# Attention and feed-forward block: TensorE takes over the last sum, GpSimd weighs two rows, gathers follow the transposes

## What is computed

```python
x = x + xattn(layernorm(x), ctx, idx, Wq, Wkv, Wo)
x = x + ffn(layernorm(x), w_gate, w_up, w_down)

def xattn(q, kv_src, seg_id, Wq, Wkv, Wo):      # 16 heads of 32
    qh = heads(q @ Wq.T)
    k, v = split(kv_src @ Wkv.T)                # 154 rows per batch
    gather = seg_id[:, :, None] - arange(4)     # 4 rows of the table per query
    k_sel, v_sel = k[clip(gather)], v[clip(gather)]
    scores = where(gather < 0, lowest, (qh * k_sel).sum(-1) / sqrt(32))
    probs = softmax(scores, over the 4 rows)
    return (probs * v_sel).sum(over the 4 rows) @ Wo.T
```

## Time and profile before

| what | us |
|---|---|
| median of 3 runs | 2348.56 |
| lowest, highest | 2347.93, 2349.85 |
| span of the profiled execution | 2347.3 |
| TensorE busy in it | 2020.4 (86%) |
| VectorE busy | 1715.7 (73%) |
| ScalarE busy | 1398.2 (60%) |
| GpSimd busy | 670.6 (29%) |

### The profile page before, as it was taken

How to read it: one execution, slowest core, us unless ns; L and a number is a source line. 1 busy time by engine, 2 the same in 40 slices (tenths; PEclk the granted TensorE clock), 3 DMA queues, 4 the chain that set the end, 5 groups by cost and what they waited for, 6 DMA issues and landing times.

```text
span 2347.3 us, 25386 instructions
## 1 busy us (share of the span) xinstructions
PE 2020.4 (86%) x9524; PEld 945.0 (40%) x9524; DVE 1715.7 (73%) x1387; ACT 1398.2 (60%) x1599; POOL 670.6 (29%) x662
## 2 busy tenths in 40 slices
PE   5888888888599999999999999999000699999998
PEld 2444444444244444444444444444000344444443
DVE  8799999999634534532499998999899644577641
ACT  4678887887422322322499996676899633366530
POOL 2599999998300000000121110222111000000000
PEclk9999999999799999999999999999555899999999
DMA  7789999998346656743699995787998755555541
GB/s 297 283 314 337 348 337 346 335 350 316 126 181 226 225 207 223 259 148 144 242 378 390 378 369 209 264 320 293 401 419 327 291 229 208 205 201 232 233 152 72
DMA packets 131162, 634.60 MB, mean 270 GB/s; under 512 B 12256, under 2 KB 12768, under 8 KB 91104
## 3 DMA queue, kind: packets, MB, share of 16 engines
q1 hardware_dynamic: 85888, 316.81, 37.0%
q0 software_dynamic: 45152, 316.16, 34.6%
HBM read 430.69 MB, written 202.24 MB: 270 GB/s over the span
## 4 chain that ended last, share of the span: by engine, by line
PE 64%; issue 3%; DVE 3%; ACT 2%; POOL 0%; DVEq 0%; ACTq 0%; POOLq 0%
PE fd_pp L1777 42%; PE fd_pp L1791 21%; ACT ff_ring L1720 1%; DVE ff_sig L1575 1%; DVE ff_h_parts L1559 1%; DVE ff_sq L1497 1%; ACT ff_sig L1707 0%; DVE ff_sq L1566 0%; DVE kept_gate L1568 0%; DVE ff_gin L1510 0%; DVE ff_hq L1549 0%; ACT ff_hq L1632 0%; ACT ff_ring L1746 0%; ACT ff_sig L1736 0%; DVE kept_o_peak L1575 0%
## 5 line engine op out<-in xcount | busy, mean ns | idle before, releaser
L1791 PE MATMUL fd_pp<-ff_down,kept_gate 128*128 128x512 f16 x1536 | 458.9, 381 | 193.1 <-DVE ff_up L1616 193.1
L1777 PE MATMUL fd_pp<-ff_h_parts,kept_gate 128*128 128x512 f16 x2304 | 499.6, 380 | 14.3 <-DVE ff_h_parts L1415 14.3
L1777 PE MATMUL fd_pp<-ff_h_parts,ff_up 128*128 128x512 f16 x2304 | 497.4, 379 | 0.0
L1639 ACT ACTIVATE ff_raw<-fd_pp 128x1024 f32<-128x1024 f32 x192 | 194.3, 1017 | 396.5 <-PE fd_pp L1777 396.5
L1777 PEld LDWEIGHTS fd_pp<-ff_h_parts,kept_gate 128*128 128x128 f16 x2304 | 225.9, 98 | 287.9 <-DVE ff_h_parts L1415 14.7
L1777 PEld LDWEIGHTS fd_pp<-ff_h_parts,ff_up 128*128 128x128 f16 x2304 | 225.4, 98 | 271.8
L1420 DVE TENSOR_REDUCE kept_gate_peak<-ff_raw 128x1 f32<-128x2048 f32 x48 | 109.7, 2285 | 292.9 <-ACT ff_raw L1639 292.9
L1791 PEld LDWEIGHTS fd_pp<-ff_down,kept_gate 128*128 128x128 f16 x1536 | 150.6, 98 | 375.9 <-issue 195.8
L1791 PE MATMUL fd_pp<-ff_down,ff_up 128*128 128x512 f16 x768 | 292.2, 380 | 0.0
L1746 ACT ACTIVATE ff_ring<-ff_hq,kept_g 128x2048 int16<-128x2048 f32 x48 | 96.0, 1999 | 191.1 <-DVE ff_hq L1549 189.7
L790 PE MATMUL at_psO<-kept_wo,at_ahi 128*128 128x512 f16 x512 | 155.5, 386 | 36.2 <-ACT at_alo L277 31.6
(11 more groups left out here) (239 smaller groups left out, 3454.9 us busy)
## 6 DMA issues: line engine op xcount, KB each, us to landing
ff_raw<-up_scratch SPq DMA_DIRECT2D x66, 1024.0 KB, 8.5
gate_scratch<-ff_raw POOLq DMA_DIRECT2D x48, 1024.0 KB, 9.1
ff_gin<-gate_scratch SPq DMA_DIRECT2D x48, 1024.0 KB, 8.7
up_scratch<-ff_raw POOLq DMA_DIRECT2D x48, 1024.0 KB, 7.7
ff_gin<-gate_integers SPq DMA_DIRECT2D x73, 512.0 KB, 5.8
gate_integers<-ff_ring POOLq DMA_DIRECT2D x43, 512.0 KB, 8.7
ff_up<-up_scratch SPq DMA_DIRECT2D x21, 1024.0 KB, 9.5
kept_xs<-in_x SPq DMA_DIRECT2D x32, 512.0 KB, 14.6
```

The source lines that it names most:

```text
L1639: nc.scalar.activation(raw[:, n % UNITS, h * 2 * BLK:(h + 1) * 2 * BLK], pp[(2 * n + h) % 4][:, :, :].rearrange("p a t -> p (a t)"), ACT.C ...
L1777: mm = nc.tensor.matmul(pp[k % 4][:, h, :], wt[w][:, c, f:f + P], a[:, b % 2, :, c, :], start=(q == 0), stop=(q == len(todo) - 1))
L1791: mm = nc.tensor.matmul(pp[k % 8 // 2][:, k % 2, :], a[b % 2][:, f, t * P:(t + 1) * P], wt[w][:, f, :], start=(q == 0 and i == 0), stop=(q ...
```

## The change

Five things change in `opening`:

- VectorE weighs rows 0 and 1 only (1024 numbers instead of 1536). GpSimd weighs rows 2 and 3 (`weigh_upper`, 1024 numbers instead of 512), still once both tiles of the pair are weighed by VectorE.
- The second sum and its buffer `att` are gone (a buffer `room` keeps the place in memory). TensorE turns both half sums into the same place in PSUM, eight transposes instead of four, the second four accumulating on the first.
- The semaphore `att` is gone. TensorE waits for `half`; SyncE and the gathers wait for `aT`, so a buffer is gathered into once TensorE has turned its tile.
- GpSimd issues the gather for the even tile before the norm's four instructions, and the one for the odd tile behind them.
- For the last pair VectorE only makes the first sum (`add_last`).

The diff:

```diff
--- before.py
+++ after.py
@@ -158,7 +158,8 @@
 
         xn = r.sb("xn", [P, 2, D], F32)
         xhi, xlo = (r.sb(n, [P, 2, DC, P], F16) for n in ("xhi", "xlo"))
-        att, hn = (r.sb(n, [P, 2, D], F32) for n in ("att", "hn"))
+        r.sb("room", [P, 2, D], F32)
+        hn = r.sb("hn", [P, 2, D], F32)
         hT = r.sb("hT", [P, 4, D], F32)
         ahi, alo = (r.sb(n, [P, 2, DC, P], F16) for n in ("ahi", "alo"))
         kv = r.sb("kv_rows", [P, KR, W, 2 * D], F32)
@@ -185,7 +186,7 @@
         x1_out = [r.sem(f"x1_out{i}") for i in range(XR)]
         hT_out = [r.sem(f"hT_out{i}") for i in range(2)]
         rows_in = [r.sem(f"rows_in{i}") for i in range(KR)]
-        m = r.sems("xn xT xhi xrest xlo q prod raw sc top ds ex tot inv pr pv last half att aT ahi arest alo o x1 "
+        m = r.sems("xn xT xhi xrest xlo q prod raw sc top ds ex tot inv pr pv last half aT ahi arest alo o x1 "
                    "nmean ssq ssq_v stat aggr sqe root rstd norm x_nmean x_ssq hn hT hT_sb peak h_red h_all reduced")
 
         def blocks(t, h):
@@ -232,7 +233,7 @@
                         sp.dma_start(x1_v[p], xs[:, ring(p), :]).then_inc(x1_out[p % XR], 16)
                     p = s_ - 5
                     if p == NP - 6:
-                        sp.wait_ge(m["att"], KR * (NT // KR) - KR + 6 if NT % KR == 0 else NT - NT % KR)
+                        sp.wait_ge(m["aT"], KR * (NT // KR) - KR + 6 if NT % KR == 0 else NT - NT % KR)
                         for b in range(2):
                             sp.wait_ge(hT_out[0], 16 * (b + 1))
                             sp.wait_ge(hT_out[1], 16 * (b + 1))
@@ -521,8 +522,8 @@
                                             AX.X, ALU.add).then_inc(m["raw"], 1)
 
                 def weigh(t):
-                    values = kv[:, t % KR, 0:W - 1, D:2 * D].rearrange("p w (h e) -> p w h e", h=H)
-                    nc.vector.tensor_tensor(values, values, pr[:, t % 2, 0:W - 1].unsqueeze(3).to_broadcast([P, W - 1, H, HD]),
+                    values = kv[:, t % KR, 0:2, D:2 * D].rearrange("p w (h e) -> p w h e", h=H)
+                    nc.vector.tensor_tensor(values, values, pr[:, t % 2, 0:2].unsqueeze(3).to_broadcast([P, 2, H, HD]),
                                             ALU.mult).then_inc(m["pv"], 1)
 
                 def residual(t):
@@ -537,15 +538,11 @@
                     nc.vector.tensor_reduce(keep["h_peak"][:, hp:hp + 1], hT[:, k:k + 2, :].rearrange("p a d -> p (a d)"),
                                             AX.X, ALU.max, apply_absolute_value=True).then_inc(m["peak"], 1)
 
-                def sum_last(t):
+                def add_last(t):
                     dve.wait_ge(m["last"], t + 1)
                     dve.wait_ge(m["pv"], t + 1)
                     nc.vector.tensor_tensor(kv[:, t % KR, 0:2, D:2 * D], kv[:, t % KR, 0:2, D:2 * D], kv[:, t % KR, 2:4, D:2 * D],
                                             ALU.add).then_inc(m["half"], 1)
-                    dve.wait_ge(m["half"], t + 1)
-                    dve.wait_ge(m["aT"], t - 1)
-                    nc.vector.tensor_tensor(att[:, t % 2, :], kv[:, t % KR, 0, D:2 * D], kv[:, t % KR, 1, D:2 * D],
-                                            ALU.add).then_inc(m["att"], 1)
 
                 def last_moments(t):
                     p, k = t // 2, t - (LAST - 3)
@@ -602,11 +599,11 @@
                         dve.wait_ge(m["pr"], s_ + 1)
                         weigh(a)
                         if s_ == NP - 1:
-                            sum_last(a)
+                            add_last(a)
                             residual(a - 2)
                         weigh(a + 1)
                         if s_ == NP - 1:
-                            sum_last(a + 1)
+                            add_last(a + 1)
 
                 h_peak(NP - 5)
                 last_moments(LAST - 3)
@@ -681,28 +678,25 @@
                                                 in_offset=bass.IndirectOffsetOnAxis(ap=keep["rows"][:, t:t + 1], axis=0),
                                                 element_offset=0).then_inc(rows_in[t % KR], 16)
 
-                def weigh_fourth(t):
-                    last = kv[:, t % KR, W - 1, D:2 * D].rearrange("p (h e) -> p h e", h=H)
+                def weigh_upper(t):
+                    upper = kv[:, t % KR, 2:4, D:2 * D].rearrange("p w (h e) -> p w h e", h=H)
                     pool.wait_ge(rows_in[t % KR], 16 * (t // KR + 1))
                     pool.wait_ge(m["pr"], t // 2 + 1)
                     if t < LAST - 1:
                         pool.wait_ge(m["pv"], t // 2 * 2 + 2)
-                    nc.gpsimd.tensor_tensor(last, last, pr[:, t % 2, W - 1].unsqueeze(2).to_broadcast([P, H, HD]),
+                    nc.gpsimd.tensor_tensor(upper, upper, pr[:, t % 2, 2:4].unsqueeze(3).to_broadcast([P, 2, H, HD]),
                                             ALU.mult).then_inc(m["last"], 1)
 
                 def add_up(t):
-                    weigh_fourth(t)
+                    weigh_upper(t)
                     lower, upper = kv[:, t % KR, 0:2, D:2 * D], kv[:, t % KR, 2:4, D:2 * D]
                     pool.wait_ge(m["last"], t + 1)
                     nc.gpsimd.tensor_tensor(lower, lower, upper, ALU.add).then_inc(m["half"], 1)
-                    pool.wait_ge(m["half"], t + 1)
-                    need(pool, m["aT"], t - 1)
-                    nc.gpsimd.tensor_tensor(att[:, t % 2, :], kv[:, t % KR, 0, D:2 * D], kv[:, t % KR, 1, D:2 * D],
-                                            ALU.add).then_inc(m["att"], 1)
 
                 def gather_next(t):
-                    pool.wait_ge(m["att"], t + 1)
-                    gather(t + KR)
+                    if tile(t) and t + KR < NT:
+                        pool.wait_ge(m["aT"], t + 1)
+                        gather(t + KR)
 
                 for t in range(KR):
                     if t == 0:
@@ -720,15 +714,16 @@
                     gather(t)
                 for s_ in range(NP + 6):
                     if s_ == NP:
-                        weigh_fourth(LAST - 1)
-                        weigh_fourth(LAST)
+                        weigh_upper(LAST - 1)
+                        weigh_upper(LAST)
                     if pair(s_ - 1) and s_ < NP:
                         add_up(2 * s_ - 2)
                         add_up(2 * s_ - 1)
                         gather_next(2 * s_ - 2)
-                        gather_next(2 * s_ - 1)
                     if s_ > 0 and (pair(s_ - 3) or pair(s_ + 3)):
                         norms(s_)
+                    if pair(s_ - 1) and s_ < NP:
+                        gather_next(2 * s_ - 1)
                 nc.gpsimd.partition_all_reduce(last_all[:, :], eps_d[:, 0:1], P, PEAK).then_inc(m["reduced"], 1)
                 pool.wait_ge(m["h_red"], 1)
                 nc.gpsimd.partition_all_reduce(h_all[:, :], h_red[:, :], P, PEAK).then_inc(m["h_all"], 1)
@@ -818,9 +813,14 @@
                     project(psQ[t % 2], xhi, xlo, wq, t % 2).then_inc(m["q"], 1)
 
                 def turn_a(t):
-                    pe.wait_ge(m["att"], t + 1)
+                    pe.wait_ge(m["half"], t + 1)
                     need(pe, m["alo"], t)
-                    turn(psA, att[:, t % 2, :]).then_inc(m["aT"], 1)
+                    for j in range(2):
+                        for c in range(DC):
+                            mm = nc.tensor.matmul(psA[:, c, :], kv[:, t % KR, j, D + c * P:D + (c + 1) * P], ident[:, :],
+                                                  is_transpose=True, start=(j == 0 and c == 0), stop=(j == 1 and c == DC - 1),
+                                                  skip_group_check=True)
+                    mm.then_inc(m["aT"], 1)
 
                 def rest_a(t):
                     pe.wait_ge(m["ahi"], t + 1)
```

## The result

The changed kernel takes 2375.47 us (median of 4 runs, 2374.94 to 2376.91), the kernel before 2348.85 (4 runs, 2347.93 to 2349.85). The ratio is 1.0116 with an interval of 1.0103 to 1.0128: 26.6 us slower. Forecast were 2370 us, slower, with a range of 2354 to 2381. The profiled execution has a span of 2373.5 us, 26.2 more than before.

A forecast was written before the change was run, and what follows sets the result against it. The attention slot was taken as a loop through VectorE and GpSimd, which hold each other. Later slots of 17.65 us put subtraction 30 21.7 us later; less 1.3, plus 1.6 tail: 22 on 2348.6, about 2370 us, range 2354 to 2381.

The forecast's parts named there:

- The two engines keep each other out: Attention slots: two-SBUF-input VectorE instructions and GpSimd instructions exclude each other; a held masking or subtraction ends 0.15 us after GpSimd's sum.
- The odd gather decides, with GpSimd's work queued behind it: GpSimd's in-order queue: the gather waits for odd transposes, so weighing starts 3 us behind VectorE, idling some 5 us a slot.
- VectorE's saving and GpSimd's weighing: Weighing in each slot: VectorE's two rows instead of three save 1.07 us; GpSimd's 1024 elements take 2.0 us.
- the second rival: GpSimd's weighing of 1024 elements costs 2.37 us like the sum; slot 17.95, 8 us more, 2378 us; chance 12%.
- The slot of 17.65: Attention slots: 17.81 us if the masking loses to GpSimd's last sum, 17.1 to 17.35 if not; 17.65 taken, for 26 slots.
- Slipping in: Masking gets in before GpSimd's last sum, so the subtraction is held instead, ending 0.15 us after it; slot 17.1 to 17.35.
- cover for its extra transposes: TensorE: 0.86 us a slot of extra transposes hidden in its 1.06 us wait; without that cover, 24 us.
- The start and the tail: Subtraction 2 ends at 114.2 us, the next two slots take 16.7 each; slot 31 gains 1.3, the tail adds 1.6.
- Landings and the norm: Odd gathers, issued 5 to 6 us later, still land in time at no cost; norm's small products take 0.2 us.
- No hold: First rival: engines don't exclude each other or only briefly; ScalarE and TensorE's loop sets the slot, about 2335 us; 11%.
- The dearer weighing: GpSimd's 1024-element weighing costs 2.37 us instead of 2.0; slot 17.95 us, 8 us more, 2378 us; chance 12%.
- Break-even: Third rival: odd transposes come about 0.7 us sooner than implied; slots of 16.9 to 17.0 us, 2346 to 2353 us; 6%.

The follow-up runs named there:

- old weights: The changed kernel with the weighing split as before (VectorE three rows, GpSimd one), its sums, transposes and gathers kept: 2343.31 us, 0.9978 of the kernel before.
- peak first: The kernel with the odd gather between GpSimd's two sums, plus VectorE taking the hidden row's peak ahead of the masking: 2325.90 us, 0.9906 of the kernel before.
- Two halves: New sums, transposes and gathers with the weighing split as before: 2343.31 us; the kernel before with only the weighing split changed to two rows each: 2351.24 us.

## Why the prediction was right, step by step

**The two engines keep each other out: right.** In each typical slot the masking ends 0.15 us after GpSimd's last sum, in each long one the subtraction does. Moving the sum away (old weights), or the masking away (peak first), brings it to 0.35.

**The odd gather decides, with GpSimd's work queued behind it: right, and shown.** Predicted were an idle time of some 5 us and a weighing 3 us behind VectorE's products; measured 4.98 and 3.1. One moved gather gives 47 us back.

**VectorE's saving and GpSimd's weighing: nearly right.** The pair of weighings took 384.35 - 382.08 = 2.27 us on VectorE (3.35 before, so 1.08; I had 1.07). GpSimd's 1024 elements took 1.92, the lower of my bounds, and not the 2.0 I took nor the 2.37 of the second rival; the rate that the Trainium skill gives ("GPSIMD Engine Reference", Elementwise), 2.6 cycles an element at 1.2 GHz and so an estimate of 2.2 us, was above it too, and below the 2.36 us of the sum of 1024 elements.

**The slot of 17.65: nearly right in the typical slot.** I had put 17.81 for a masking that loses the race for the last sum and 17.1 to 17.35 for one that slips in, and mixed them. In the typical slot it loses, 17.73. That is the 17.81 less 0.16 for the two cheaper weighings, and some 0.1 more because the gather starts 0.28 us behind the end of the transposes (386.39 against 385.07 + 1.04) and not 0.16. So 17.65 came close partly by luck: what I took off for cases that slip in was, in fact, the cheaper weighing.

**Slipping in: right where it came, but not where I put it.** In slots 3 to 5, in which VectorE doesn't yet take the hidden row's peak, the masking got in ahead of the last sum as worked out, held at most by the second weighing. Slot 5, on VectorE:

```profile
160.20 1.05 DVE L571 SCALAR_TENSOR_TENSOR at_sc<-at_sc,kept_alpha,kept_mask 128x128 f32<-128x128 f32 x1
161.69 2.00 DVE L581 TENSOR_TENSOR at_sc<-at_sc,at_top 128x128 f32<-128x128 f32 x1
```

That slot took 17.01 us, near my 17.1. With the peak in the slot GpSimd's sum wins every time, unless the clock makes GpSimd late, and then the slot is 18.69: the shorter case that I mixed into the steady slots is not among them.

**TensorE's clock: missing.** No step of mine had it, since the clock was 1.00 in the stretch that I read before. I counted TensorE's waits as cover for its extra transposes and did not ask what such waits do to the clock. Six of 25 slots are longer by it, 5.7 us, and the experiment with four more matmuls took them away (5.7 to 6.2 us). This is the largest mis-sized term. That it is also about the whole of the 5 us between forecast and result is luck: the other errors, listed below, are up to 2 us each and nearly cancel.

**The start and the tail.** Subtraction 2 ended at 112.24, below even my lower end of 112.7: both masking and subtraction were held there, but only 1.86 and 1.48 us long, the one by the first sum and the other by the second weighing, so neither waited for the last sum, which ended at 114.52. The next two slots took 34.4 us instead of 33.4. From the subtraction of slot 30 to the end of the stage I had 0.3 more than before, measured 0.8 less; the two last weighings took 4.75 us (I had 4.9):

```profile
631.91 4.75 POOL L687 TENSOR_TENSOR at_kv_rows<-at_kv_rows,at_pr 128x1024 f32<-128x1024 f32 x2 [3.83 <-DVE at_pr L597]
```

In sum, against the 22 us forecast at the end of the stage: start -2.0, slots 3 and 4 +1.0, the other 26 slots +7.0 (nineteen of 17.73 give +1.5, six long ones +6.2, one of 17.0 takes 0.6), tail -1.1. That is 26.9, and 27.0 is measured.

**Landings and the norm.** No gather came late (12.5 us at most from 390 to 560 us). The norm's last two products take 0.20 us each. Both as predicted.

**The rivals.** No hold, 2335 us: out, in every slot. Its figure of 16.24 for the ScalarE and TensorE loop was good, though: with the gather moved, that loop sets 16.18. The dearer weighing: out (1.92). Break-even: out; TensorE's transposes follow the subtraction by what was worked out.

## What to carry to other kernels

A wait moved to a later event is not priced by its own engine's slack but by what is queued behind the waiting instruction: GpSimd had 5 us of idle time a slot, and still 0.43 us less of that wait made the slot 0.43 us shorter, since its next work, and by the hold VectorE's, stood behind. In the other direction the price was not even: 1.76 us more cost 1.02. Two halves that are harmless alone (-5.0 and +2.9 us) gave +26.6 together, so a change with two parts should be measured in each part. And when VectorE reads as full while slots get longer, compare the length of its small two-input instructions with their free length before calling it the bound.

## What was not expected of the hardware

- TensorE's granted clock fell to 0.50 in 6 of 25 slots, after it had been busy 1.97 us of four in the one shown. But the same two idle times of about 1 us are in every slot: from 378.42 to 382.42 TensorE was busy 1.98 us too, and the clock stayed at 1.00. The kernel with the transposes of the sums first still has the wait of 1.06 us, its other one is 0.7 us, and there the clock stayed at 1.00 throughout. What picks the six slots is open; that filling one of the gaps removes them is shown.
- A hold costs differently by which instruction is caught. 1.7 us later on GpSimd was worth 0.95 to 1.0 us of slot, both by the clock and by the moved norm; where both came together, the slot was even shorter than with the moved norm alone (17.7 to 18.1 us instead of 18.74), as neither instruction waited for the last sum.
- Gathers landed in 10.8 us (median) where they are issued apart, against 12.3 before, where two are issued back to back, with a DMA share of 0.92 and 0.93. Other transfers differ too, so the spacing as the cause is argued and not shown.
